# First cross attention: value products of two key tiles in every second step, the fourth key chunk one step later

## What is computed

```python
ci = rms_norm(hidden_states, ln_post_cross_w)
cq = heads(ci @ cq_w, NH, CHD)               # NH 16 heads of CHD 8 channels
ck, cv = jnp.split(encoder_outputs @ ckv_w, 2, axis=-1)
ck, cv = (heads(ck, NH, CHD), heads(cv, NH, CHD))
scores = jnp.einsum('bhqd,bhkd->bhqk', cq / sqrt(CHD), ck)    # 256 x 1601 per head
p = softmax(scores)
cctx = jnp.einsum('bhqk,bhkd->bhqd', p, cv)
hidden_states = hidden_states + cctx @ cdense_w
```

## Time and profile before

| | us |
|---|---|
| Time, median of 3 runs | 3588.94 (3585.99 to 3601.11) |
| The profiled execution, its own time | 3598.37 |
| Its span, first to last instruction | 3596.6 |
| This stage, first value product to last sum of `av` | 442.0 to 1229.8 |
| Mean granted TensorE clock | 0.972 |

### The profile page before, as it was taken

How to read it: one execution, slowest core, us unless ns; L and a number is a source line. 1 busy time by engine, 2 the same in 40 slices (tenths; PEclk the granted TensorE clock), 3 DMA queues, 4 the chain that set the end, 5 groups by cost and what they waited for, 6 DMA issues and landing times. The chain is left out here.

```text
span 3596.6 us, 74086 instructions
## 1 busy us (share of the span) xinstructions
PE 3336.7 (93%) x25176; PEld 2361.3 (66%) x25176; DVE 1947.5 (54%) x3261; ACT 1812.1 (50%) x3374; POOL 1570.7 (44%) x1421
## 2 busy tenths in 40 slices
PE   7798799998999799989999999999999998999997
PEld 5555544444444388866777677777777776878886
DVE  4465577777777354535555555555555552114444
ACT  2254276666767534435555555555555553333332
POOL 3213022122111011115777777777777785005554
PEclk9899899999999899989999999999999999999998
DMA  4785200000000222230010100010101003210200
GB/s 121 172 126 119 87 7 18 17 18 17 18 18 26 97 76 101 94 127 7 14 34 14 33 13 32 14 33 13 33 29 44 13 13 130 84 66 1 99 7 12
DMA packets 74753, 179.39 MB, mean 50 GB/s; under 512 B 14720, under 2 KB 44928, under 8 KB 68480
## 3 DMA queue, kind: packets, MB, share of 16 engines
q1 hardware_dynamic: 70240, 161.81, 15.0%
q0 software_dynamic: 4128, 12.60, 1.4%
HBM read 115.09 MB, written 59.26 MB: 48 GB/s over the span
## 5 line engine op out<-in xcount | busy, mean ns | idle before, releaser
L1813 DVE TENSOR_REDUCE cross_partmax<-cross_r 128x1 f32<-128x400 f32 (+1 forms) x1024 | 541.0, 569 | 315.7 <-PE cross_r L1897 300.2
L1657 POOL TENSOR_TENSOR cross_acc<-cross_acc,cross_probs 128x512 f32<-128x512 f32 x448 | 573.8, 1281 | 153.4 <-ACT cross_probs L1722 123.0
L1256 DVE TENSOR_REDUCE cross_partmax<-cross_m 128x2 f32<-128x800 f32 (+1 forms) x512 | 496.9, 991 | 184.7 <-PE cross_m L1359 183.6
L1722 ACT ACTIVATE cross_probs<-cross_s,cross_bias 128x512 f32<-128x512 f32 x576 | 354.4, 686 | 412.2 <-PE cross_s L1927 398.9
L1167 ACT ACTIVATE cross_probs<-cross_s 128x512 f32<-128x512 f32 (+1 forms) x832 | 453.5, 595 | 148.7 <-PE cross_s L1379 148.3
L1657 POOL TENSOR_TENSOR cross_acc<-cross_acc,cross_w 128x512 f32<-128x512 f32 (+1 forms) x256 | 327.2, 1278 | 70.1 <-ACT cross_w L1722 51.3
L1802 DVE TENSOR_TENSOR cross_k_lo<-cross_r,cross_k_hi 128x400 fp32r<-128x400 f32 (+1 forms) x256 | 147.1, 575 | 317.1 <-ACT cross_k_hi L1698 317.0
L1106 POOL TENSOR_TENSOR cross_diag<-c_ident,cross_negmax 128x256 fp32r<-128x256 f32 x128 | 75.8, 613 | 494.0 <-DVE cross_negmax L1264 494.0
L1940 PE MATMUL cross_av<-cross_probs,cross_v 128*64 128x256 f32 x2304 | 291.0, 388 | 0.0
L1390 PE MATMUL cross_av<-cross_probs,cross_v 128*32 128x256 f32 (+1 forms) x3328 | 269.0, 395 | 10.0 <-ACT cross_probs L1167 8.4
L1921 PE MATMUL cross_s<-cross_q_hi,cross_k_hi 64*128 64x256 f32 (+1 forms) x1664 | 251.4, 286 | 0.0
(11 more groups left out here) (311 smaller groups left out, 6984.1 us busy)
## 6 DMA issues: line engine op xcount, KB each, us to landing
d_masked_ctx<-tail_ctx_split SPq DMA_DIRECT2D x8, 1602.0 KB, 5.3
d_self_qk<-selfproj_qk_split POOLq DMA_DIRECT2D x32, 256.0 KB, 5.5
self_qs<-d_self_qk SPq DMA_DIRECT2D x64, 128.0 KB, 9.0
self_ks<-d_self_qk SPq DMA_DIRECT2D x64, 128.0 KB, 9.4
d_cross<-tail_pr SPq DMA_DIRECT2D x8, 1024.0 KB, 4.6
cross_qp<-d_cross SPq DMA_DIRECT2D x64, 128.0 KB, 2.3
d_cross<-cross_out SPq DMA_DIRECT2D x64, 128.0 KB, 1.8
tail_attn<-d_cross SPq DMA_DIRECT2D x8, 1024.0 KB, 5.4
```

The costliest lines, as they stand in the source:

```text
L1256: nc.vector.tensor_reduce(partmax[:, :, jt // 2, jt % 2, i:i + 1], m_pair(sets[q], w), AX.X, ALU.max).then_inc(maxed, 1)
L1657: nc.gpsimd.tensor_tensor(acc[0:w, g % 2], left, prob(t)[0:w], ALU.add).then_inc(added, 1)
L1722: nc.scalar.activation(prob(t)[0:w], src_, ACT.Exp, scale=XHD ** -0.5, bias=bias[0:w, p, t:t + 1]).then_inc(probs_ready, 1)
L1813: nc.vector.tensor_reduce(partmax[:, m, i:i + 1], r_ps[banks[q]][:, 0:KCH[i][1]], AX.X, ALU.max).then_inc(maxed, 1)
```

## The change

A table `values_at` says which value products are issued in step t: in steps 2, 4, ..., 12 those of tiles t-1 and t, one directly behind the other, in step 13 that of tile 13 (tile 0 of the next unit), in the odd steps 1 to 11 none. The products and their number stay the same. The fourth key chunk, `(1, 1)`, moves from step 6 to step 7, and with it (one step behind, by `t - 1 in k_at`) its high part on ACT and its low part on DVE, from step 7 to step 8. No transfer is touched.

```diff
--- before.py
+++ after.py
@@ -1036,7 +1036,9 @@
         FREED = {2: 1, 3: 3, 5: 4, 6: 6, 7: 7, 8: 8, 9: 9, 10: 10, 11: 11, 12: 12, 13: 13, 14: 14}
         M_SET_AHEAD = tuple(q % 2 for q in range(NM))
         K_SET, K_SET_AHEAD, V_SET, SHIFT_SET, SUM_SET = (1, 1), (0, 1), (0, 1), 1, 1
-        k_at, v_at, shift_at = {2: (0, 0), 3: (0, 1), 5: (1, 0), 6: (1, 1)}, 4, 11
+        k_at, v_at, shift_at = {2: (0, 0), 3: (0, 1), 5: (1, 0), 7: (1, 1)}, 4, 11
+        values_at = {t: (t - 1, t) for t in range(2, KT, 2)}
+        values_at[KT] = (KT,)
 
         def tile(u, nxt, step):
 
@@ -1466,7 +1468,6 @@
                     b, p, g, n = u
                     after = nxt and following(nxt, NG)
                     for t in range(1, KT + 1):
-                        now = tile(u, nxt, t)
                         soon = tile(u, nxt, t + 1)
                         items = max_at.get(t, ()) if nxt else ()
                         later = max_after_at.get(t, ()) if after else ()
@@ -1483,8 +1484,9 @@
                             key_item(nxt, after, *k_at[t])
                         for q in later[:first]:
                             max_after_item(nxt, after, q)
-                        if now:
-                            values(now)
+                        for made in values_at.get(t, ()):
+                            if tile(u, nxt, made):
+                                values(tile(u, nxt, made))
                         for q in items[1:]:
                             max_item(nxt, after, q)
                         if nxt and nxt[2] == 0 and t == v_at:
```

## The result

The changed kernel takes 3669.76 us (median of 4 runs, 3664.58 to 3674.02) where the kernel before takes 3593.48 (4 runs, 3585.99 to 3601.11): 1.0216 times as long, 95% interval 1.0194 to 1.0239. That is 76 us, where 3629 was forecast, with a range from 3607 to 3648. The direction was right; the loss forecast was 40 us, about half of the measured one.

What follows compares the result with a forecast made beforehand. PE and DVE were taken to wait on each other, the order inside a unit deciding; per unit -0.23 + 1.12 + 0.44 = +1.33, over 30 units 39.9 us, taking the median from 3588.9 to 3629 us, range 3607 to 3648.

Steps and rivals of the forecast that it cites:

- The walk: Step-by-step timing of one unit from measured spacings at full clock; plain units start 25.0 us apart, +1.33 us each.
- the first half shorter by 0.23: Steps 1 to 8, pairs in steps 2, 4 and 6: M14 at 13.35 us, before 13.58; -0.23 us per unit.
- the low part ahead of M15: Steps 7 to 8: M15 waits for the fourth key chunk's low part on DVE, +1.12 us per unit.
- V(11) and V(12) ahead of copy_av: Step 12: both products stand between S(13) and copy_av; add_shift to copy_av 2.50 us instead of 2.06, +0.44 per unit.
- a second product 0.44: In each pair: a product right behind another takes 0.44 us instead of 0.57, 0.13 saved.
- the sum has 1.33: Whole unit: -0.23 + 1.12 + 0.44 = +1.33 us per unit, 39.9 us over 30 units.
- The rival that PE is the bound: Whole stage: six pairs save 0.13 us each in 31 units, 24 us faster, 3565 us; chance 0.07.
- the rival that the first half runs at its set's pace: Steps 1 to 7: M14 at 12.1 us, 1.25 earlier than walked; +0.08 per unit, 3591 us; chance 0.08.
- part 1: Pairs in steps 2, 4 and 6: 0.57 us leaves each odd step but gives little; first half 0.23 us shorter.
- step 2: First pair's step: S(3) at 1.54 us, M8 at 2.80 as before, S(4) at 4.90, before 4.48.
- Units 30 and 31: Last two units of the stage, without a key chunk: counted at no change.

Runs made afterwards that it cites:

- the fill: Changed kernel with five matmuls of constants added ahead of M7 and five ahead of M8, where PE waits, results never read: 3651.02 us, ratio 1.0146.

## Why the prediction was wrong in size

**The order of work: right, to some hundredths.** The walk had a plain unit at 25.04 and it is 25.14. By its parts: the first half shorter by 0.23 (measured M14 13.37 against 13.58, 0.21); the low part ahead of M15 +1.12 (2.09 against 0.95 from start to start, +1.14); V(11) and V(12) ahead of copy_av +0.44 (2.58 against 2.06, +0.52); a second product 0.44 (0.43). The runs with one part each confirm the parts of the chunk and of V(11): 24.88 with the chunk alone moved, 24.66 with V(11) back. Over the units without a fall it is 1.31 per unit, in the trace with the fill against the one of before, where the sum has 1.33. The parts are not prices that can be had back one by one: with the pairs in place, taking the chunk back gives 0.24 per unit, as the walk for that run had it, and not 1.12. The rival that PE is the bound fell with the pairs of tiles 3 to 10 (1.0021); the rival that the first half runs at its set's pace wanted M14 at 12.1, and it stands at 13.37.

**What failed** is the sentence in part 1 by which 0.57 is removed from each odd step and "gives little", and step 2's "S(3) right behind M7 at 1.54, M8 2.80 as before". That M8 is not later is true. I costed the emptied step at nothing, and had no term for the clock in the sum. The work that was removed there had a use that no timeline of before shows as a wait: it kept PE busy between two waits, in the one part of the unit where PE has nothing else to do. With it gone, PE is busy 2.46 to 2.62 of the 4.37 us from the sum to the first key chunk (3.21 before), the granted clock falls in 19 of 29 units instead of 4, and the products behind the fall run at half the clock for 1.5 us of loss. That is 25.3 us by the trace with the fill. The idle to ask about was in the rows of before: 0.84 us ahead of M7 in the earlier trace rows.

**Units 30 and 31** were counted at nothing, and cost 5.4 us, of which 3.1 are left in the trace with the fill (39.3 us there against 36.2); what of the unit they are was not looked into.

**The rest of the distance.** The profiled executions differ by 67.5 us: 40.2 order (with some 2 of remaining falls), 25.3 clock, 5.4 the last two units, 9.0 ahead of the first sum, 12.4 less behind the stage. Of the 9.0, 2.7 lie behind the first value product, in unit 0, which the forecast counts among its 30. The other 6.3 and the 12.4 I cannot tie to the change. The experiments' traces have the first sum anywhere from 470.9 to 480.4, and the part behind the stage from 2355.5 to 2377.3. Of the 41 us between the forecast and the measured median, 4.5 are the median of before, 3588.94 then and 3593.48 with one more run.

**What stays open:** how the clock is decided in a single unit. With V(1) in its place and the other waits added, 8 units fell (4 before), with the chunk's wait alone 4, and with V(11) back 14 instead of 19. Whether the load elsewhere in the unit plays a part, these single traces do not separate from chance.

## What to carry to other kernels

When a product is moved away from between two waits, ask what is left for TensorE in that stretch, even if nothing waits for the product: the engine's clock can depend on it. Pairing matmuls saved some 0.14 each on TensorE where the pair ran unbroken and bought nothing here, where the unit waits for other engines; one maximum moved to the other set, found by walking the chain of waits, took 0.96 off each unit, more than the 0.8 that all six pairs could have given. And a read by one engine that frees a buffer for another (here the low part ahead of M15) has to be moved with an eye on who is behind it in both queues.

## What the runs showed of the hardware

In plain units of the changed kernel the granted clock fell to its lower level although PE was never idle for longer than 0.9 us at a time from the sum to the first key chunk; it did 2.5 to 2.6 us of work in these 4.4 where they passed at full clock. The kernel before did 3.2 of 4.4 there and had 4 falls in 29 units; the one with the fill did 4.0 and had 2, both in units 8 and 16, where PE stands still for more than 3 us; the changed kernel with M7 in the other set did 2.6 of 3.3 and had the same 2. More idle in another place (the chunk's wait alone) added no fall. Ten matmuls of constants, whose results nobody reads, kept the clock at no cost to the order of work.

The Trainium skill, TensorE: Matmul & The Clock Gate, advises under Why this matters for your kernels to leave no long gaps between bursts of matmuls, lest the clock fall. The traces here agree: where PE stood still for over 3 us, in units 8 and 16, all eleven show a fall. But no long gap was needed: in the 17 other units of the changed kernel that have one, gaps of 0.9 us at most, close together, were enough.
